# A mixture of experts whose tiles gather their rows: inverse slot map by one-hot products, W1 as the stationary operand, layer norms batch by batch

## The chip, the cores and the metric

The kernel runs on one core of a Trainium2 chip. The metric is the device time of one launch in microseconds (us). A core has five engines that run their own instruction streams in order and meet at semaphores: TensorE (PE), VectorE (DVE), ScalarE (ACT), GpSimd (POOL) and SyncE (SP), which here only issues DMAs. An engine that waits holds up all that stands behind the wait in its own stream.

## The reference

An audio tower of two layers over 8 sequences. The first stage keeps 16 of each 128 tokens, which leaves 8 x 512 = 4096 tokens of D = 128 numbers. Then (cut to what matters):

```python
h = h + L0_attn(layernorm(h), ...)          # gated retention
h = h + L0_ffn(layernorm(h), ...)           # experts, top 1
h = h + L1_attn(layernorm(h), video, ...)   # cross-attention
h = h + L1_ffn(layernorm(h), ...)           # experts, top 2

# L0_ffn: E = 8 experts, F = 512, one expert for each token, gate 1
logits = xf @ Wr + br;  idx = top_1(logits)
out[token] = relu(xf @ W1[idx] + b1[idx]) @ W2[idx] + b2[idx]

# L1_ffn: two experts for each token, gates = softmax of the two logits
h_e = relu(xf @ w1[e] + b1[e]) @ w2[e] + b2[e]
y_e = (xf + h_e - mean) * rsqrt(var + 1e-6) * gamma[e] + beta[e]
out[token] = gate_1 * y_e1 + gate_2 * y_e2
```

## The kernel before

The 4096 tokens lie in SBUF as G = 32 groups of 128 (`hidden`). The stages run one after the other with a barrier between them: the choice of tokens, `project` and the rest of the retention, the first mixture (moe1), the norm of the cross-attention (`crossnorm`) and the attention itself, the second mixture (moe2), and the end.

Both mixtures are one function, `route_and_mix`. Its first block, the **route**, takes the layer norm, the router's logits, the top 1 or 2, and the slot of each token: slots are grouped by expert and rounded up to tiles of 128, so that a tile has one expert. There are 40 tiles in moe1 and 72 in moe2. Then GpSimd scatters the 32 groups of normed rows (64 in moe2, once for each choice) to a DRAM table `routed`, in slot order, by indirect DMAs (L1064). Slots without a token need a row too, so `zero_dram` fills both tables with zeros earlier, during `project`. A row carries the slot of the output and the gate as two more columns.

`LayerNorm` works in phases: `statistics` of all 32 groups on VectorE (L201, L205), one power of 32 columns on GpSimd (L154), then `batch` for batch (L218). It is used by `project`, both routes and `crossnorm`.

The second block, the **mix**, runs the tiles. The ring holds RING = 8 tiles; SyncE loads pairs of tiles from `routed` (L1230), each pair as soon as the results that lay in its places are out, so up to eight tiles ahead. Every engine runs the tiles in an unrolled turn of 8, with the experts' numbers read into registers at a turn's start (`experts`). TensorE is in order. In its step t it transposes the rows of tile t+1 into `psX` (`turn_rows`, L1283), takes the first product of tile t into `psH` (L1278: the rows stationary, 512 columns of W1 moving), transposes the hidden numbers of tile t-1 into `psF` (L1288), and takes the second product of tile t-2 into `psY` (L1297). VectorE copies `psH` to `hid` (L1368), and in moe2 does `begin` of tile t-2 (L1382 to L1388: bias, residual, statistics) and `finish` of tile t-3 (L1395 to L1398), which sets `result_ready`. ScalarE copies the transposed rows (L1336) and does bias and relu (L1342). GpSimd takes the power of moe2's norm (L154) and scatters each result to DRAM (L1244).

The order on TensorE and on VectorE is what the steps of the prediction rest on:

```python
# TensorE, step t                    # VectorE, step t (moe2)
turn_rows(t + 1)                     # hidden_copy(t)
first_product(t)                     # begin(t - 2)   needs second_product(t - 2)
turn_hidden(t - 1)                   # finish(t - 3)  sets result_ready
second_product(t - 2)
```

## Time and profile before

| what | us |
|---|---|
| median of 2 runs (3289.16 and 3291.8) | 3290.48 |
| span of the profiled execution | 3251.5 |
| outside the span (the profiled execution's own time is taken as the median: 3290.48 - 3251.5) | 39.0 |
| PE busy | 2491.1 (77%) |
| DVE busy | 2290.4 (70%) |
| POOL busy | 1794.4 (55%) |
| ACT busy | 1729.9 (53%) |
| moe1: route with norm, scatter, mix | 53, 44, 140 |
| moe2: route with norm, scatter, mix | 55, 90, 336 |
| cross-attention after its norm | 1826 |

The span is the time from the first to the last instruction of one profiled execution. The shares are means over stages that stand apart by barriers, so the two mixtures have to be read by themselves: a window from a stage's start to its end gives the busy time of each engine there. PEclk is TensorE's granted clock as a share of its upper level: 0.50 is 1.2 GHz, 1.00 is 2.4 GHz. In a timeline, [x <-y] is the idle time of the engine before the row and what ended it; "issue" is a wait for nothing that the profile shows.

### The profile page before, as it was taken

The page shows a single profiled execution, that of the slowest core. Times are in us where ns is not written, and L with a number is a line of the kernel's source. Part 1 is how long each engine was busy: PE and PEld are TensorE (multiplying, and loading weights), DVE is VectorE, ACT ScalarE, POOL GpSimd, SP SyncE. Part 2 cuts the span into 40 slices and gives each one's busy share as a digit, 9 for nine tenths or more (in the row PEclk, how much of TensorE's full clock was granted, in tenths as well). Part 3 has the DMA queues.
Part 4 walks back from the last instruction along what each step waited for, and adds up shares of the span by engine and source line. Part 5 has one row for each costly group of instructions (what it writes and reads, how often), then busy time and mean ns, then how long its engine had stood idle before and what let it go on. Part 6 is the DMA issues. An engine that isn't in the chain of part 4 may idle for free. (4 is left out here: it accounts for less than half of the span.)

```text
span 3251.5 us, 57608 instructions
## 1 busy us (share of the span) xinstructions
PE 2491.1 (77%) x15032; PEld 2097.6 (65%) x15033; DVE 2290.4 (70%) x5410; ACT 1729.9 (53%) x3648; POOL 1794.4 (55%) x1986
## 2 busy tenths in 40 slices
PE   5441077528489999999999999999999997326663
PEld 3220055426368988898898889889888986214442
DVE  6624633413479999999999999999999997225664
ACT  2123122204257777777777777777777775113331
POOL 2325500133257777777777777777777775343332
PEclk8665555558789999999999999999999999568887
DMA  6260000211100000000000000000000001110103
GB/s 210 73 110 0 0 1 0 59 33 38 48 1 1 0 0 0 0 0 0 0 0 0 0 0 0 0 0 0 0 0 0 0 0 60 38 41 27 31 30 93
DMA packets 88587, 72.49 MB, mean 22 GB/s; under 512 B 21600, under 2 KB 75872, under 8 KB 88544
## 3 DMA queue, kind: packets, MB, share of 16 engines
q1 hardware_dynamic: 70480, 51.49, 6.3%
q0 software_dynamic: 7680, 15.84, 1.4%
q10 hardware_dynamic: 10384, 4.66, 0.5%
q8 instruction: 18, 0.29, 0.0%
q14 instruction: 25, 0.20, 0.0%
HBM read 48.66 MB, written 23.30 MB: 22 GB/s over the span
## 5 line engine op out<-in xcount | busy, mean ns | idle before, releaser
L1810 POOL TENSOR_TENSOR attend_weights<-attend_weights,attend_scales 128x512 f32<-128x512 f32 x1024 | 1068.9, 1044 | 499.5 <-DVE attend_scales L1721 471.9
L1713 DVE TENSOR_REDUCE attend_maxima<-attend_psL 128x8 fp32r<-128x512 f32 x1030 | 706.9, 686 | 146.0 <-PE attend_psL L1591 146.0
L1770 ACT ACTIVATE attend_highT<-attend_psT 128x512 fp32r<-128x512 f32 x1024 | 556.2, 595 | 261.9 <-PE attend_psT L1605 261.9
L1717 DVE TENSOR_REDUCE attend_sums<-attend_weights 128x8 f32<-128x512 f32 x1029 | 653.2, 635 | 3.2 <-ACT attend_weights L1766 3.2
L1766 ACT ACTIVATE attend_weights<-attend_psL 128x512 f32<-128x512 f32 x1029 | 615.9, 599 | 11.1 <-PE attend_psL L1595 11.1
L1605 PE MATMUL attend_psT<-consts,attend_weights 128*128 128x128 f32 x4096 | 530.4, 272 | 0.0
L1605 PEld LDWEIGHTS attend_psT<-consts,attend_weights 128*128 128x128 f32 x4096 | 479.1, 140 | 70.4 <-issue 0.2
L1615 PE MATMUL attend_psA<-attend_highT,attend_chunk_values 128*128 128x256 f32 x2048 | 515.6, 285 | 1.6
L1615 PE MATMUL attend_psA<-attend_lowT,attend_chunk_values 128*128 128x256 f32 x2048 | 513.6, 282 | 0.0
L1595 PE MATMUL attend_psL<-attend_maxima,neg_ident 128*128 128x512 f32 x1029 | 434.0, 422 | 3.9 <-DVE attend_maxima L1713 3.9
L1590 PE MATMUL attend_psL<-keys,attend_q_high 128*128 (+1 forms) x1030 | 411.1, 399 | 8.8 <-PE attend_psA L1615 7.2
L1591 PE MATMUL attend_psL<-keys,attend_q_low 128*128 (+1 forms) x1030 | 406.8, 395 | 0.0
L1615 PEld LDWEIGHTS attend_psA<-attend_lowT,attend_chunk_values 128*128 128x128 f32 x2048 | 389.4, 190 | 13.1
L1615 PEld LDWEIGHTS attend_psA<-attend_highT,attend_chunk_values 128*128 128x128 f32 x2048 | 389.9, 190 | 8.1 <-issue 8.1
L1774 ACT ACTIVATE attend_lowT<-attend_psT 128x512 fp32r<-128x512 f32 x512 | 306.4, 598 | 146.2 <-PE attend_psT L1641 146.2
L1725 DVE TENSOR_TENSOR attend_lowT<-attend_psT,attend_highT 128x512 fp32r<-128x512 f32 x512 | 348.7, 681 | 6.0 <-ACT attend_highT L1770 6.0
L1590 PEld LDWEIGHTS attend_psL<-keys,attend_q_high 128*128 128x128 f32 x1030 | 194.0, 188 | 58.7 <-issue 10.2
L1591 PEld LDWEIGHTS attend_psL<-keys,attend_q_low 128*128 128x128 f32 x1030 | 194.5, 189 | 37.1
L1641 PE MATMUL attend_psT<-attend_highT,neg_ident 128*128 128x512 f32 x512 | 202.6, 396 | 0.0
L1595 PEld LDWEIGHTS attend_psL<-attend_maxima,neg_ident 128*128 128x128 f32 x1029 | 195.2, 190 | 7.5 <-DVE attend_maxima L1713 7.5
L1721 DVE RECIPROCAL attend_scales<-attend_sums 128x8 f32<-128x8 f32 x1028 | 198.3, 193 | 0.0
L1824 POOL TENSOR_TENSOR attend_chunk_values<-values,attend_chunk_values 128x256 fp32r<-128x256 f32 x256 | 189.4, 740 | 0.0
(299 smaller groups left out, 3081.4 us busy)
## 6 DMA issues: line engine op xcount, KB each, us to landing
select_xbuf<-in_x_dram SPq DMA_DIRECT2D x16, 1024.0 KB, 5.4
routed<-project_zeros SPq DMA_DIRECT2D x14, 520.0 KB, 11.3
moe2mix_rows<-routed SPq DMA_DIRECT2D x36, 130.0 KB
select_emb<-L_attn_video_embeds_dram ACTq DMA_DIRECT2D x16, 256.0 KB, 2.9
moe2back_back<-result SPq DMA_DIRECT2D x8, 512.0 KB, 7.2
moe1mix_rows<-routed SPq DMA_DIRECT2D x20, 130.0 KB, 2.2
moe_w<-in_L_ffn_W_dram SPq DMA_DIRECT2D x1, 2048.0 KB, 10.8
moe1back_back<-result SPq DMA_DIRECT2D x4, 512.0 KB, 6.2
```

The costliest lines, as they stand in the source:

```text
L1590: pe.matmul(psL[:, s, :], q_high[h][:, tile], K.keys[:, ds(key, KC)], start=True, stop=False, skip_group_check=True)
L1591: pe.matmul(psL[:, s, :], q_low[h][:, tile], K.keys[:, ds(key, KC)], start=False, stop=False, skip_group_check=True).then_inc(logits_ready, 1)
L1595: pe.matmul(videos(psL[:, s, :]), K.neg_ident[:], maxima[:, s, :, None].to_broadcast([P, VC, FR]), start=False, stop=True, skip_group_chec ...
L1605: mm = pe.matmul(psT[:, side, at:at + P], weights[:, w + t, k * P:(k + 1) * P], ident, is_transpose=True, start=(at == 0), stop=False, ski ...
L1615: mm = pe.matmul(psA[:, j * 2 * P:(j + 1) * 2 * P], value, part[:, half, side, at], start=False, stop=(k == SUB - 1), skip_group_check=True)
L1713: dve.tensor_reduce(maxima[:, s, :], videos(psL[:, s, :]), X, ALU.max).then_inc(maxima_ready, 1)
L1717: dve.tensor_reduce(sums[:, w, :], videos(weights[:, w, :]), X, ALU.add).then_inc(summed, 1)
L1725: dve.tensor_tensor(lowT[:, half, LEFT, :], psT[:, LEFT, :], highT[:, half, LEFT, :].bitcast(F32), ALU.subtract).then_inc(left_lows, 1)
L1766: act.activation(weights[:, w, :], psL[:, w % TB, :], ACT.Exp, scale=float(DH1) ** -0.5).then_inc(exped, 1)
L1770: act.activation(highT[:, half, side, :], psT[:, side, :], ACT.Copy).then_inc(highs, 1)
L1774: act.activation(lowT[:, half, RIGHT, :], psT[:, RIGHT, :], ACT.Copy).then_inc(right_lows, 1)
L1810: pool.tensor_tensor(w, w, scales[:, s, :, None].to_broadcast([P, VC, FR]), ALU.mult).then_inc(normalised, 1)
```

## The change

It has three parts.

**Layer norms.** `statistics` and `batch` give way to `batches`: for each batch of four groups the statistics, the square, a power of four columns on GpSimd and the scaling, with the statistics of the next batch ahead of the scaling of this one. All four users take it. In `project` the wait for the weights now stands ahead of the norm.

**The route.** No row is scattered and nothing is filled with zeros. SyncE writes the normed table to DRAM in token order, by four plain DMAs (in moe2 behind the gates, which are its last two columns). Which token sits in which slot is found on the chip: for each four groups VectorE makes one-hots of the tile (`tile_token`, which carries the token's number) and of the lane (`lane_hot`), and TensorE multiplies them into `psI`, over 8 such parts in moe1 and 16 in moe2. Some operations on `psI` give `source` (the row to gather), `target` (the row of the result) and `second` (which of the two gates).

**The mix.** GpSimd gathers the rows of a tile from the table (L1225) and scatters the results (L1233). EARLY = 5 tiles are gathered first; the gather of tile t+5 stands behind the scatter of tile t, which waits for its result. SyncE loads nothing. ScalarE copies the tile's W1 (128x512) to `w1_tile`, TensorE takes the first product with W1 stationary in four matmuls, whose output is already transposed, so `psF`, `hid` and their copy are gone. In moe2 a fifth matmul of the second product adds the residual, the root is ScalarE's Sqrt with a reciprocal on VectorE, and the gate comes by one more small operation (L1374).

```diff
-        pool.wait_ge(self.square_ready, 1)
-        inverse_root(pool, K, self.root[:], self.square[:]).then_inc(self.root_ready, 1)
...
+        for b in range(B):
+            part = slice(b * TB, (b + 1) * TB)
+            pool.wait_ge(self.square_ready, b + 1)
+            inverse_root(pool, K, self.root[:, part], self.square[:, part]).then_inc(self.root_ready, 1)
+    def batches(self, dve, hidden, rows, ready, ring=B, used=None):
+        for b in range(B + 1):
+            if b < B:
+                for g in range(b * TB, (b + 1) * TB):
+                    dve.bn_stats(self.stats[:, g, :], hidden[:, g, :]).then_inc(self.steps, 1)
+            if b > 0:
+                dve.wait_ge(self.root_ready, b)
+                if used and b > ring:
+                    dve.wait_ge(used, b - ring + 2)
+                for g in range((b - 1) * TB, b * TB):
+                    ins = dve.tensor_scalar(rows[:, g % (ring * TB), 0:D], hidden[:, g, :], self.mv[:, g, 0:1], self.root[:, g:g + 1],
+                                            ALU.subtract, ALU.mult)
+                ins.then_inc(ready, 1)
+            if b < B:
+                dve.wait_ge(self.steps, b * 2 * TB + TB)
+                for g in range(b * TB, (b + 1) * TB):
+                    dve.bn_aggr(self.mv[:, g, :], self.stats[:, g, :]).then_inc(self.steps, 1)
+                dve.wait_ge(self.steps, (b + 1) * 2 * TB)
+                part = slice(b * TB, (b + 1) * TB)
+                dve.tensor_scalar(self.square[:, part], self.mv[:, part, 1], self.scale, self.eps, ALU.mult, ALU.add).then_inc(self.square_ready, 1)
...
+                    table = K.normed_dram[top].rearrange("(g p) d -> p g d", p=P)
+                    if last:
+                        sp.wait_ge(shares_kept, 2)
+                    for q in range(4):
+                        part = slice(q * (G // 4), (q + 1) * (G // 4))
+                        sp.wait_ge(norm_ready, 2 * (q + 1))
+                        sp.dma_start(table[:, part, :], normed[:, part, :]).then_inc(table_out, 16)
+                    sp.wait_ge(table_out, 64)
...
-                    pool.wait_ge(rows_kept, B + 2)
-                    for k in range(top):
-                        pool.wait_ge(slots_ready, k + 1)
-                        pool.wait_ge(tagged, 2 * (k + 1))
-                        for g in range(G):
-                            pool.indirect_dma_start(K.routed_dram[top], bass.IndirectOffsetOnAxis(ap=slots[:, k, g:g + 1], axis=0),
...
+                    for i in range(parts):
+                        k, n = i // (G // PART), i % (G // PART)
+                        pe.wait_ge(lanes_ready, i + 1)
+                        pe.wait_ge(tokens_ready, PART * (i + 1))
+                        for j in range(PART):
+                            mm = pe.matmul(psI[:, k, 0:tiles], lane_hot[:, i % HOTS, j, :], tile_token[:, i % HOTS, j, :],
+                                           start=(n == 0 and j == 0), stop=(n == G // PART - 1 and j == PART - 1))
+                        mm.then_inc(hots_used, 1)
...
+                    for i in range(parts):
+                        if i >= HOTS:
+                            dve.wait_ge(hots_used, i - HOTS + 1)
+                        for j in range(PART):
+                            c = i * PART + j
+                            dve.tensor_scalar(tile_token[:, i % HOTS, j, :], K.const("lane")[:, 0:tiles], tile_of[:, c:c + 1],
+                                              K.const("token1")[:, c % G:c % G + 1], ALU.is_equal, ALU.mult).then_inc(tokens_ready, 1)
+                        dve.tensor_tensor(lane_hot[:, i % HOTS], K.const("lane")[:, None, :].to_broadcast([P, PART, P]),
+                                          lane_of[:, i * PART:(i + 1) * PART, None].to_broadcast([P, PART, P]), ALU.is_equal).then_inc(lanes_ready, 1)
...
+                    spare = K.const("spare")[:, 0:tiles]
+                    dve.wait_ge(hots_used, parts)
+                    steps.then(dve.tensor_copy(token1[:], psI[:, 0, 0:tiles]))
+                    if last:
+                        steps.mark(dve.tensor_scalar(second[:], psI[:, 1, 0:tiles], 1.0, None, ALU.min))
+                        steps.then(dve.tensor_tensor(token1[:], psI[:, 1, 0:tiles], token1[:], ALU.add))
+                    steps.mark(dve.tensor_scalar(source[:], token1[:], -1.0, 0.0, ALU.add, ALU.max))
+                    steps.then(dve.tensor_scalar(filled[:], token1[:], 1.0, None, ALU.min))
+                    if last:
+                        steps.then(dve.scalar_tensor_tensor(token1[:], second[:], float(N), token1[:], ALU.mult, ALU.add))
+                    steps.then(dve.scalar_tensor_tensor(token1[:], token1[:], float(SPARE - 1), spare, ALU.add, ALU.subtract))
+                    steps.then(dve.tensor_tensor(token1[:], token1[:], filled[:], ALU.mult))
+                    steps.then(dve.tensor_tensor(target[:], token1[:], spare, ALU.add))
...
-            RING, PAIR = 8, 2
+            RING, EARLY = 8, 5
...
+                    def gather(t):
+                        pool.indirect_dma_start(rows[:, t % RING, :], None, K.normed_dram[top],
+                                                bass.IndirectOffsetOnAxis(ap=source[:, t:t + 1], axis=0)).then_inc(rows_in[t % RING], 16)
+                    for t in range(EARLY):
+                        gather(t)
+                    for t in range(tiles):
+                        pool.wait_ge(result_ready, t + 1)
+                        pool.indirect_dma_start(K.result_dram[top], bass.IndirectOffsetOnAxis(ap=target[:, t:t + 1], axis=0),
+                                                result[:, t % RING, :], None).then_inc(result_out[t % RING], 16)
+                        if t + EARLY < tiles:
+                            if t + EARLY >= RING:
+                                pool.wait_ge(result_out[(t + EARLY) % RING], 16 * ((t + EARLY) // RING))
+                            gather(t + EARLY)
...
-                    def first_product(t, s, e):
-                        pe.matmul(psH[:, s % 2, :], rowsT[:, s % 2, :], w1[:].rearrange("p e f -> p (e f)")[:, ds(e * F, F)],
-                                  start=True, stop=True).then_inc(hid_ready, 1)
...
+                    def first_product(t, s, bank_used):
+                        pe.wait_ge(w1_copied, t + 1)
+                        if bank_used:
+                            pe.wait_ge(hidT_done, t - 1)
                         for c in range(FC):
-                            mm = pe.transpose(psF[:, s % 2, c * P:(c + 1) * P], hid[:, s % 2, c * P:(c + 1) * P], ident)
-                        mm.then_inc(hidT_ready, 1)
+                            part = slice(c * P, (c + 1) * P)
+                            mm = pe.matmul(psH[:, s % 2, part], w1_tile[:, s % 2, part], rowsT[:, s % KEEP, :],
+                                           start=True, stop=True, skip_group_check=True)
+                        mm.then_inc(hid_ready, 1)
...
+                        if last:
+                            mm = pe.matmul(psY[:, s % 2, 0:D], rowsT[:, s % KEEP, :], ident, start=False, stop=True)
                         mm.then_inc(mixed_ready, 1)
...
+                        act.activation(rowsT[:, s % KEEP, :], psX[:, s % 2, 0:P], ACT.Copy).then_inc(rowsT_copied, 1)
+                        act.activation(w1_tile[:, s % 2, :], w1[:].rearrange("p e f -> p (e f)")[:, ds(e * F, F)], ACT.Copy).then_inc(w1_copied, 1)
+                    def activate(t, s, e, used):
+                        act.wait_ge(hid_ready, t + 1)
+                        if used:
+                            act.wait_ge(mixed_ready, t - 1)
...
+                            ins = act.activation(hidT[:, s % 2, c * P:(c + 1) * P], psH[:, s % 2, c * P:(c + 1) * P], ACT.Relu,
                                                  bias=flat[:, ds(e + c * E, 1)])
                         ins.then_inc(hidT_done, 1)
+                    def deviation(t, s):
+                        if last:
+                            act.wait_ge(square_ready, t + 1)
+                            act.activation(root[:, s % 2:s % 2 + 1], square[:, s % 2:s % 2 + 1], ACT.Sqrt).then_inc(root_ready, 1)
...
-                        dve.wait_ge(rows_in[s // PAIR], 16 * it + 16)
-                        steps.then(dve.tensor_tensor(res, rows[:, s, 0:D], of_expert(b2, e), ALU.add))
-                        dve.wait_ge(mixed_ready, t + 1)
-                        steps.then(dve.tensor_tensor(res, mixed, res, ALU.add))
+                        ins = dve.tensor_tensor(res, mixed, of_expert(b2, e), ALU.add)
+                        ins.then_inc(mixed_used, 1)
+                        dve.wait_ge(mixed_used, t + 1)
...
                         res = result[:, s, :]
+                        dve.wait_ge(root_ready, t + 1)
+                        steps.mark(dve.reciprocal(inverse[:], root[:, s % 2:s % 2 + 1]))
+                        steps.mark(dve.scalar_tensor_tensor(scale[:, s % 2:s % 2 + 1], second[:, ds(t, 1)], rows[:, s, D + 1:D + 2], rows[:, s, D:D + 1], ALU.mult, ALU.add))
                         steps.then(dve.scalar_tensor_tensor(res, res, mv[:, s % 2, 0:1], of_expert(gamma, e), ALU.subtract, ALU.mult))
-                        dve.wait_ge(root_ready, t + 1)
-                        steps.then(dve.scalar_tensor_tensor(res, res, root[:, s % 2:s % 2 + 1], of_expert(beta, e), ALU.mult, ALU.add))
-                        dve.tensor_scalar(res, res, rows[:, s, D + 1:D + 2], None, ALU.mult).then_inc(result_ready, 1)
+                        steps.then(dve.scalar_tensor_tensor(res, res, inverse[:], of_expert(beta, e), ALU.mult, ALU.add))
+                        dve.tensor_scalar(res, res, scale[:, s % 2:s % 2 + 1], None, ALU.mult).then_inc(result_ready, 1)
```

In the order of the built program one sees what stands in a row. The first place is GpSimd's stream in the mix of moe2, before (`result` at the left is the table of results in DRAM):

```order
L1244 DMA result<-moe2mix_result,moe2mix_rows 9216x128
L154 TENSOR_TENSOR moe2mix_root<-moe2mix_square,consts 128x1
L1244 DMA result<-moe2mix_result,moe2mix_rows 9216x128
L154 TENSOR_TENSOR moe2mix_root<-moe2mix_square,consts 128x1
L1244 DMA result<-moe2mix_result,moe2mix_rows 9216x128
L154 TENSOR_TENSOR moe2mix_root<-moe2mix_square,consts 128x1
```

and after, from the start of that block (`normed` is the table in DRAM, `moe2mix_rows` the ring of tiles):

```order
L1225 DMA moe2mix_rows<-normed,moe_source 128x130 x5
L1233 DMA result<-moe2mix_result,moe_target 9216x128
L1225 DMA moe2mix_rows<-normed,moe_source 128x130
L1233 DMA result<-moe2mix_result,moe_target 9216x128
L1225 DMA moe2mix_rows<-normed,moe_source 128x130
L1233 DMA result<-moe2mix_result,moe_target 9216x128
L1225 DMA moe2mix_rows<-normed,moe_source 128x130
```

The powers have left GpSimd; five gathers come first, and each later gather stands behind a scatter.

The second place is TensorE's step in the mix of moe2, before (an ISA row sets an address from a register):

```order
L1283 MATMUL moe2mix_psX<-consts,moe2mix_rows 128x128
L1278 ISA
L1278 MATMUL moe2mix_psH<-moe_w,moe2mix_rowsT 128x512
L1288 MATMUL moe2mix_psF<-consts,moe2mix_hid 128x128 x4
L1292 REGISTER_ALU
L1295 REGISTER_ALU
L1297 ISA
L1297 MATMUL moe2mix_psY<-moe_w,moe2mix_hidT 128x128
L1297 ISA
L1297 MATMUL moe2mix_psY<-moe_w,moe2mix_hidT 128x128
```

and after:

```order
L1247 MATMUL moe2mix_psX<-consts,moe2mix_rows 128x128
L1256 MATMUL moe2mix_psH<-moe2mix_rowsT,moe2mix_w_tile 128x128 x4
L1266 ISA
L1266 MATMUL moe2mix_psY<-moe_w,moe2mix_hidT 128x128
L1266 ISA
L1266 MATMUL moe2mix_psY<-moe_w,moe2mix_hidT 128x128
L1266 ISA
L1266 MATMUL moe2mix_psY<-moe_w,moe2mix_hidT 128x128
L1266 ISA
L1266 MATMUL moe2mix_psY<-moe_w,moe2mix_hidT 128x128
L1271 MATMUL moe2mix_psY<-consts,moe2mix_rowsT 128x128
```

The row of `psX` still stands ahead of everything else of its step; the four transposes are gone, the first product has four rows, and the second product ends with a fifth (L1271).

The third place is VectorE's step in the mix of moe2, before:

```order
L1368 COPY moe2mix_hid<-moe2mix_psH 128x512
L1382 ISA
L1382 TENSOR_TENSOR moe2mix_result<-moe2mix_rows,moe_b 128x128
L104 REGISTER_ALU
L1384 TENSOR_TENSOR moe2mix_result<-moe2mix_psY,moe2mix_result 128x128
L104 REGISTER_ALU
L1385 BN_STATS moe2mix_stats<-moe2mix_result 128x6
L104 REGISTER_ALU
L110 MEMSET moe2mix_pause 128x1
L1387 BN_AGGR moe2mix_mv<-moe2mix_stats 128x2
L104 REGISTER_ALU
L1388 TENSOR_SCALAR moe2mix_square<-moe2mix_mv 128x1
```

and after:

```order
L1359 TENSOR_TENSOR moe2mix_result<-moe2mix_psY,moe_b 128x128
L1362 BN_STATS moe2mix_stats<-moe2mix_result 128x6
L106 REGISTER_ALU
L112 MEMSET moe2mix_pause 128x1
L1364 BN_AGGR moe2mix_mv<-moe2mix_stats 128x2
L106 REGISTER_ALU
L1365 TENSOR_SCALAR moe2mix_square<-moe2mix_mv 128x1
L1373 RECIPROCAL moe2mix_inverse<-moe2mix_root 128x1
L1374 ISA
L1374 SCALAR_TENSOR_TENSOR moe2mix_scale<-moe_second,moe2mix_rows 128x1
L1375 REGISTER_ALU
L1375 SCALAR_TENSOR_TENSOR moe2mix_result<-moe2mix_result,moe2mix_mv,moe_gamma 128x128
```

The copy of the hidden numbers and the row of rows and bias (L1382) are gone; the reciprocal and the scale stand at the head of `finish`, which still comes behind the next tile's `begin`.

## Rows read from the trace of the kernel before

**Rows 1.** Busy time by stage; columns: us, PE, PEld, DVE, ACT, POOL, PEclk, DMA, GB/s

```profile
625.00:678.00 53.00, 24.56 (x160) 23.58 (x160) 27.01 (x121) 8.92 (x16) 5.73 (x2) 0.53 0.35 90
678.00:722.00 44.00, 0.00 (x0) 0.00 (x0) 0.20 (x2) 0.00 (x0) 30.46 (x32) 0.50 0.15 48
722.00:862.00 140.00, 105.42 (x600) 78.71 (x600) 39.35 (x80) 53.51 (x200) 46.68 (x80) 0.87 0.14 41
870.00:904.00 34.00, 8.92 (x32) 5.72 (x32) 19.95 (x98) 4.78 (x8) 5.46 (x1) 0.50 0.00 0
2747.00:2802.00 55.00, 24.89 (x160) 23.92 (x160) 29.53 (x130) 9.16 (x17) 5.42 (x1) 0.53 0.37 106
2802.00:2892.00 90.00, 0.00 (x0) 0.00 (x0) 3.02 (x9) 0.00 (x0) 61.38 (x64) 0.50 0.14 47
2892.00:3228.00 336.00, 213.92 (x1080) 148.60 (x1080) 192.83 (x720) 101.18 (x360) 115.17 (x144) 0.87 0.09 29
2998.80:3035.40 36.60, 25.11 (x121) 17.52 (x120) 21.47 (x80) 11.24 (x40) 12.80 (x16) 0.83 0.09 29
```

**Rows 2.** Timeline around the two scatters of rows; columns: start us, length us

```profile
677.69 1.07 POOL L1064 DMA_INDIRECT routed<-moe1route_normed,moe_slots  x1 [34.30 <-DVE moe_slots L1178]
...
716.95 0.96 POOL L1064 DMA_INDIRECT routed<-moe1route_normed,moe_slots  x1 [0.31 <-issue]
...
724.83 0.45 PE L1283 MATMUL moe1mix_psX<-consts,moe1mix_rows 128*128 128x128 f32 x1 [51.54 <-DMA moe1mix_rows<-routed]
...
2894.70 0.45 PE L1283 MATMUL moe2mix_psX<-consts,moe2mix_rows 128*128 128x128 f32 x1 [96.60 <-DMA moe2mix_rows<-routed]
```

**Rows 3.** Timeline of VectorE in moe1's layer norm and first routing step

```profile
625.93 1.01 DVE L201 BATCH_NORM_STATS2 moe1norm_stats<-hidden  x4 [1.18 <-PEq L176]
...
635.28 2.40 DVE L205 BATCH_NORM_AGGREGATE moe1norm_mv<-moe1norm_stats 128x2 f32<-128x6 f32 x32
...
643.88 2.30 DVE L218 TENSOR_SCALAR moe1norm_rows<-hidden,moe1norm_mv,moe1norm_root 128x128 f32 x8 [5.99 <-POOL moe1norm_root L154]
...
665.54 0.42 DVE L1121 TENSOR_TENSOR moe1route_logits<-moe1route_psR,moe1route_router_bias 128x256 f32<-128x256 f32 x1 [5.66 <-PE moe1route_psR L1085]
```

**Rows 4.** Timeline of TensorE in one turn of moe1's mix

```profile
751.71 0.47 PE L1283 MATMUL moe1mix_psX<-consts,moe1mix_rows 128*128 128x128 f32 x1 [4.54 <-issue]
...
753.71 1.06 PE L1288 MATMUL moe1mix_psF<-consts,moe1mix_hid 128*128 128x128 f32 x4
754.56 1.92 PE L1297 MATMUL moe1mix_psY<-moe_w,moe1mix_hidT 128*128 x8
...
759.07 0.27 PE L1283 MATMUL moe1mix_psX<-consts,moe1mix_rows 128*128 128x128 f32 x1
...
760.04 0.60 PE L1288 MATMUL moe1mix_psF<-consts,moe1mix_hid 128*128 128x128 f32 x4
760.48 1.06 PE L1297 MATMUL moe1mix_psY<-moe_w,moe1mix_hidT 128*128 x8
```

**Rows 5.** Timeline of one step of moe2's mix, all engines

```profile
2970.11 0.29 DVE L1384 TENSOR_TENSOR moe2mix_result<-moe2mix_psY,moe2mix_result 128x128 f32<-128x128 f32 x1 [0.71 <-PE moe2mix_psY L1297]
...
2971.95 0.29 DVE L1398 TENSOR_SCALAR moe2mix_result<-moe2mix_result,moe2mix_rows 128x128 f32<-128x128 f32 x1
...
2972.15 0.68 DVE L1368 COPY moe2mix_hid<-moe2mix_psH 128x512 f32<-128x512 f32 x1
2972.39 0.57 POOL L154 TENSOR_TENSOR moe2mix_root<-moe2mix_square,consts 128x1 f32<-128x1 f32 x1 [1.83 <-DVE moe2mix_result L1398]
...
2972.47 1.13 PE L1297 MATMUL moe2mix_psY<-moe_w,moe2mix_hidT 128*128 x8 [1.06 <-DVE moe2mix_result L1398]
...
2973.71 0.29 DVE L1384 TENSOR_TENSOR moe2mix_result<-moe2mix_psY,moe2mix_result 128x128 f32<-128x128 f32 x1 [0.68 <-PE moe2mix_psY L1297]
```

**Rows 6.** Waits in moe2's mix; columns: total us, times, longest

```profile
PE moe2mix_psY L1297 <- DVE moe2mix_result L1398: 46.5, 49, 3.0
```

**Rows 7.** Indirect DMA of moe2's mix, the view of the tile moe2mix_rows

```profile
DMA to landing us min/median/max: 2.2/2.3/3.5
```

313 lines of the change are left out of this document (110 added, 203 removed).

## Prediction

> **What bounds the kernel now.** I read the busy time by stage first [rows 1], because the whole-span shares (PE 77%) come mostly from the 1826 us of attention, which the change leaves alone. Four kinds of stage remain. In the routes (53 and 55 us) no engine is busy more than about half the time: a chain of small steps. In the two scatters (44 and 90 us) only GpSimd works, and everybody waits for it. In the mixes TensorE leads: 105.4 of 140 us in moe1; in moe2 213.9 of 336, with VectorE at 192.8. The timeline of a mix step [rows 5] shows why neither reaches its span in moe2: the second product waits for `result_ready` (the wait L1297 <- L1398 holds 46.5 us in 49 cases [rows 6]) and VectorE then waits for the product. The rows themselves are never late inside the mix, since SyncE loads them up to eight tiles ahead. This is the cover that I watch below.
>
> **Layer norms.** Before, in moe1's route: 32 statistics from 625.93, 32 aggregates in 2.40, a GpSimd power (5.99 idle), then scaling at 2.30 for 8, with waits, and the first logits step at 665.54: 39.6 us [rows 3]. After, VectorE needs for each batch 1.01 (statistics) + 0.30 (an eighth of 2.40) + about 0.2 (square) + 1.15 (half of 2.30) + about 0.45 for waits at semaphores = 3.1; the power of four columns lies beside the next batch's statistics. 8 x 3.1 = 24.8, and behind the last batch about 4 of the 5.66 us that VectorE waits there now: 28.8. That is -11, and the same in moe2. `crossnorm` and `project` have the same norm, but TensorE and ScalarE pace their batches and `project` now waits for its weights first: -7 each, an estimate, bounds 0 and -11. Sum -36. The zero fills lie beside `project` and cost or save nothing on the path.
>
> **Scatters become one-hots.** A scatter comes every (716.95 - 677.69) / 31 = 1.27 us, and the mix begins at 724.83, 47.1 after the first [rows 2]. Instead, each part costs VectorE one 128x512 operation (0.68, as L1368 [rows 5]) and four small ones on 128x40 or 128x72. Their price has no row; below it lies an aggregate's 0.075, above it 0.29 for 128x128 [rows 5]. I take 0.19 and 0.22, nearer the upper row: 1.44 and 1.55 a part, 11.5 us for 8 and 24.8 for 16 (bounds 7.8 to 14.7, and 15.7 to 29.4). The four matmuls of a part lie beside the next part; if each cost a quarter of the slow second product (1.92 / 4 = 0.48 [rows 4]) they would be the pace at 1.92, +4 and +6. Around them stand 0.8 for the digits, 1.3 for the owners, 1.6 (moe1) and 3.0 (moe2) for the tail, 1.2 for the block's change and 2.5 for the first gather. The slots are known 0.9 before moe1's first scatter (677.69 [rows 2]) and at about 2802.4 in moe2 [rows 1]. moe1's first `psX` comes at 676.8 - 0.5 + 0.8 + 11.5 + 1.3 + 1.6 + 1.2 + 2.5 = 695.2 against 724.83: -29.6. moe2's comes at 2802.4 + 0.9 + 24.8 + 1.3 + 3.0 + 1.2 + 2.5 = 2836.1 against 2894.70: -58.6. The table's write ends beside the one-hots. All savings: -124.
>
> **The mix of moe2, where the gathers now stand.** Loads left SyncE, which had nothing else to do, and stand in GpSimd's stream, one gather behind one scatter. Follow a tile. The gather of tile r+5 is issued after the scatter of tile r, and that waits for result r. Result r is `finish` in VectorE's step r+3, behind `begin` of tile r+1 in the same step. `begin` needs the second product of tile r+1, which TensorE does in its step r+3, behind `turn_rows` of tile r+4. So the rows of r+5 are not even requested until the rows of r+4 have arrived and gone through three engines. Five early tiles are exactly as many as one result needs; none is left to run ahead. TensorE's wait for rows holds its first and second products; VectorE, ScalarE and GpSimd wait behind those. One tile costs one whole round:
>
> - result to scatter 0.15 (the next GpSimd step starts at 2972.39, L1398 ends at 2972.24 [rows 5]); scatter to gather 1.27 [rows 2];
> - gather to landing 2.5: an indirect DMA here has 2.2 / 2.3 / 3.5 [rows 7], and a gather reads before it writes, so I go a little above the median; bounds 2.2 and 3.5;
> - TensorE's step, with a hand-over of 0.1 before and after. At the clock's upper level a step lasts from 759.07 to 761.54, 2.47 us, less 0.44 for `psF` (760.04 to 760.48) = 2.03, and the fifth matmul adds 0.27: 2.3. At the lower level it lasts from 751.71 to 756.48, 4.77, less 0.85 for `psF` (753.71 to 754.56) = 3.92, plus 0.43: 4.35 [rows 4];
> - VectorE from L1384 at 2970.11 to the end of L1398 at 2972.24: 2.13 [rows 5], plus 0.25 for reciprocal and scale: 2.4.
>
> The round is 0.15 + 1.27 + 2.5 + 0.1 + 4.35 + 0.1 + 2.4 = 10.9 us at the lower level and 8.8 at the upper. The registers' loads at a turn's start (4.54 idle in [rows 4]) now lie inside the wait, as does all of ScalarE's added work: the copy of W1 lies beside the wait for rows, and uncovered it would cost about 0.6 a tile, 43 us in all. Which level? The clock was granted at 0.53 and 0.50 in the stages where TensorE works less than half the time (24.6 of 53, 8.9 of 34) and at 0.83 in a mix turn with 25.1 of 36.6 [rows 1]; the new step keeps it busy 4.35 of 10.9 or 2.3 of 8.8. The step after a wait of 4.54 us ran at the lower level [rows 4], and each new step follows a wait of 6.5. I take the lower.
>
> The Trainium skill, page "TensorE: Matmul & The Clock Gate", section "HAM oscillation — how this bites in real kernels", says that where the matmuls of each tile are shorter than the wait for its data, the clock drops in every wait and each tile starts cold. The step after the idle 4.54 us agrees [rows 4]. By that rule moe2's mix would go at 10.9 a tile; without it at 8.8.
>
> Before: 9 turns x 36.6 = 329 [rows 1]. After: 67 rounds x 10.9 = 730, some 15 until the first result and 12 for the last four tiles = 757. So +428 (at the upper level 67 x 8.8 + 24 = 614, +285).
>
> **The mix of moe1.** The result is set in `begin` of step r+2, so it needs the rows of r+3 and not of r+4: two tiles share a round. At the lower level 3.92 + 0.1 + 0.29 + 0.2 + 1.27 + 2.5 + 0.1 = 8.4 for two, at the upper 6.5. 17.5 rounds = 147, ends 12, uncovered turn loads 4: 163, against 140 - 12 = 128 [rows 1]. +35 (upper level about +5).
>
> One table load for Sqrt on ScalarE is under 2 us. **Sum**, from the profiled 3251.5 + 39.0 = 3290.5, which is the median: -124 + 35 + 428 = 3630.
>
> **Rivals.**
> - *A, the forecast: lockstep, lower clock*, 3630. For it: the order of the three streams, and the clock rows.
> - *B: lockstep, but the clock stays at its upper level*: -124 + 5 + 285 = 3457 to 3470. For it: mix stages had 0.87 as a mean. Against: that was with TensorE busy two thirds of the time.
> - *C, the other side: no lockstep*. If five tiles in flight cover the round trip, each tile takes what the busiest engine needs: GpSimd two DMAs, 2.54, VectorE 2.4, TensorE 2.3. Then moe2 goes at moe1's old pace, 9 x 26.2 + 12 = 248 (-77; 26.2 is moe1's turn of 8, (140 - 9) / 5 [rows 1]), moe1 -9, and the kernel takes 3080. The place is the gather's start: it needs gather r+5 to be issued while tile r+4 is still under way. The point from which it decides: the change is slower once moe2 pays over (124 + 329) / 72 = 6.3 us a tile, and DMAs, TensorE and VectorE in series are above that even with every lower bound (0.15 + 1.27 + 2.2 + 2.3 + 2.1 = 8.0). Against it: in-order streams leave no way past the wait.
> - *D: the table does not do what it says*, with gathers at the slow end, 3.5 a landing: +67, 3700.
>
> **Chances.** A 0.62, B 0.20, C 0.07, D 0.04; the rest (a clock between the levels, a partly broken chain) 0.07, mostly slower. The range takes in A, B's upper part and the gather's bounds: 3455 to 3700. Faster by over 2% (about what a measurement can tell from no change) 0.07, within 2% 0.02, slower 0.91.
>
> **What would show it.** In moe2's mix L1247 starts about 10.9 apart, each behind a wait for the DMA of `moe2mix_rows` of 6 us or so; L1233 waits for VectorE's L1377; PEclk is near 0.5; the first `psX` of moe2's mix comes some 58 us sooner after the route's start plus 11. In moe1's mix the rows arrive in pairs. The forecast is wrong if TensorE's waits for those DMAs are short, or if PEclk in the mix is near 1.

## The result and the profile after

The changed kernel took 3602.13 us (median of 3577.7 and 3626.56) against 3290.48: a ratio of 1.099, 95% interval 1.074 to 1.125. The profiled execution took 3577.7 us with a span of 3575.8. Executions of one kernel fall into two groups some 40 us apart (before: 3246 to 3261 or 3279 to 3296), by TensorE's clock in the `project` stage, which the last section shows; both profiled executions, before and after, had the higher clock there, so their spans, 3251.5 and 3575.8, are compared below: +324.3.

The windows of the stages after the change answer to [rows 1] (same columns: us, busy of PE, PEld, DVE, ACT and POOL, PEclk, DMA share, GB/s). They are moe1's norm, its route behind the norm, its mix; the norm of the cross-attention; the same three of moe2; and eight tiles in the middle of moe2's mix:

```profile
612.40:640.00 27.60, 21.18 (x96) 20.12 (x96) 19.17 (x107) 4.78 (x8) 8.07 (x8) 0.50 0.87 232
640.00:669.40 29.40, 12.65 (x96) 11.32 (x96) 20.36 (x71) 0.00 (x0) 2.00 (x2) 0.56 0.06 18
669.40:833.80 164.40, 99.48 (x680) 93.79 (x680) 11.66 (x40) 75.35 (x240) 76.23 (x78) 0.88 0.12 32
853.50:879.00 25.50, 8.92 (x32) 5.72 (x32) 19.28 (x105) 4.78 (x8) 8.09 (x8) 0.50 0.00 0
2722.00:2749.70 27.70, 21.17 (x96) 20.11 (x96) 19.27 (x108) 4.78 (x8) 8.08 (x8) 0.55 0.75 210
2749.70:2797.50 47.80, 21.55 (x128) 18.89 (x128) 39.19 (x129) 0.23 (x1) 2.07 (x3) 0.54 0.24 46
2797.50:3547.50 750.00, 282.47 (x1368) 267.72 (x1368) 144.87 (x720) 148.57 (x505) 138.82 (x142) 0.63 0.05 13
3100.00:3184.00 84.00, 31.96 (x152) 30.29 (x152) 14.90 (x73) 15.14 (x51) 15.65 (x16) 0.62 0.05 13
```

The scatter stages are gone (29.5 and 47.9 us lie between the logits and the first rows in place of 59.3 and 107.6), and moe2's mix has grown to 750 us, in which no engine is busy even 40% of the time. TensorE's clock there is 0.63, where it was 0.87 [rows 1]. The timeline shows one tile of moe2's mix:

```profile
3101.24 0.99 POOL L1233 DMA_INDIRECT result<-moe2mix_result,moe_target  x1 [8.62 <-DVE moe2mix_result L1377]
3102.53 0.97 POOL L1225 DMA_INDIRECT moe2mix_rows<-normed,moe_source  x1 [0.30 <-issue]
...
3105.06 0.48 PE L1247 MATMUL moe2mix_psX<-consts,moe2mix_rows 128*128 128x128 f32 x1 [6.52 <-DMA moe2mix_rows<-normed,moe_source]
...
3105.33 1.92 PE L1256 MATMUL moe2mix_psH<-moe2mix_rowsT,moe2mix_w_tile 128*128 128x128 f32 x8
...
3107.03 1.91 PE L1266 MATMUL moe2mix_psY<-moe_w,moe2mix_hidT 128*128 x8
...
3108.74 0.64 PE L1271 MATMUL moe2mix_psY<-consts,moe2mix_rowsT 128*128 128x128 f32 x2
...
3109.52 0.29 DVE L1359 TENSOR_TENSOR moe2mix_result<-moe2mix_psY,moe_b 128x128 f32<-128x128 f32 x1 [8.56 <-PE moe2mix_psY L1271]
...
3111.51 0.29 DVE L1377 TENSOR_SCALAR moe2mix_result<-moe2mix_result,moe2mix_scale 128x128 f32<-128x128 f32 x1
3112.07 0.99 POOL L1233 DMA_INDIRECT result<-moe2mix_result,moe_target  x1 [8.57 <-DVE moe2mix_result L1377]
```

From one scatter to the next are 10.83 us. They go: scatter and gather issued 1.29 apart, rows used at 3105.06 (2.53 after the gather), TensorE until 3109.38, VectorE until 3111.80, and 0.27 to the next scatter. No two of these overlap. Before, a step took 3.60 (L1384 to L1384 [rows 5]). The view of waits in the same stage (engine and instruction, what it waited for, total us, times, longest) shows all engines in it:

```profile
DVE moe2mix_result L1359 <- PE moe2mix_psY L1271: 586.6, 69, 14.6
POOL result L1233 <- DVE moe2mix_result L1377: 579.8, 71, 12.0
PE moe2mix_psX L1247 <- DMA moe2mix_rows<-normed,moe_source: 462.7, 68, 8.0
```

The gathers themselves are nearly as fast as the scatters (the view of `moe2mix_rows`, where [rows 7] had 2.2, 2.3 and 3.5 for the scatters):

```profile
DMA to landing us min/median/max: 2.4/2.5/3.6
```

In moe1 the scatters come in pairs, two tiles to a round (GpSimd's timeline; the gathers between them are left out). The first round shown, from 688.13 to 694.86, lasts 6.73; the next, which holds the register loads at a turn's start, 10.54:

```profile
688.13 0.99 POOL L1233 DMA_INDIRECT result<-moe1mix_result,moe_target  x1 [3.50 <-DVE moe1mix_result L1356]
...
690.70 0.99 POOL L1233 DMA_INDIRECT result<-moe1mix_result,moe_target  x1 [0.30 <-issue]
...
694.86 0.99 POOL L1233 DMA_INDIRECT result<-moe1mix_result,moe_target  x1 [1.89 <-DVE moe1mix_result L1356]
...
697.48 0.98 POOL L1233 DMA_INDIRECT result<-moe1mix_result,moe_target  x1 [0.36 <-issue]
...
705.40 0.99 POOL L1233 DMA_INDIRECT result<-moe1mix_result,moe_target  x1 [5.66 <-DVE moe1mix_result L1356]
```

Stage by stage, from the first to the last instruction named:

| stretch | before | after | difference | forecast |
|---|---|---|---|---|
| start to moe1's norm | 625.9 | 612.7 | -13.2 | -7 |
| moe1's norm to its logits | 39.6 | 27.3 | -12.3 | -11 |
| moe1's logits to the first `psX` | 59.3 | 29.5 | -29.8 | -29.6 |
| moe1's mix, first `psX` to last scatter | 128.1 | 163.3 | +35.2 | +35 |
| to the norm of the cross-attention | 18.0 | 21.2 | +3.2 | 0 |
| that norm to the attention's first product | 33.7 | 25.6 | -8.1 | -7 |
| attention, to moe2's norm | 1842.9 | 1842.8 | -0.1 | 0 |
| moe2's norm to its logits | 39.6 | 27.3 | -12.3 | -11 |
| moe2's logits to the first `psX` | 107.6 | 47.9 | -59.7 | -58.6 |
| moe2's mix | 325.2 | 748.8 | +423.6 | +428 |
| the end | 31.6 | 29.4 | -2.2 | 0 |

### The profile page after: what moved, and what is told of

Its sections match the earlier page's. It is cut to its first block and busy times, and to the rows that moved or that the text cites. A ratio compares the mean times of both kernels' runs of the same rounds, so it can differ in the third digit from the quotient of the medians.

```text
span 3575.8 us, 57595 instructions
## 1 busy us (share of the span) xinstructions
PE 2567.8 (72%) x15496; PEld 2243.6 (63%) x15497; DVE 2255.1 (63%) x5536; ACT 1791.8 (50%) x3817; POOL 1770.4 (50%) x1917
## 5 line engine op out<-in xcount | busy, mean ns | idle before, releaser
L1359 DVE TENSOR_TENSOR moe2mix_result<-moe2mix_psY,moe_b 128x128 f32<-128x128 f32 x72 | 21.0, 291 | 588.3 <-PE moe2mix_psY L1271 586.6
L1247 PE MATMUL moe2mix_psX<-consts,moe2mix_rows 128*128 128x128 f32 x72 | 32.4, 450 | 465.3 <-DMA moe2mix_rows<-normed,moe_source 462.7
L1233 POOL DMA_INDIRECT result<-moe2mix_result,moe_target x72 | 71.1, 987 | 590.0 <-DVE moe2mix_result L1377 579.8
L1247 PEld LDWEIGHTS moe2mix_psX<-consts,moe2mix_rows 128*128 128x128 f32 x72 | 13.2, 183 | 479.5 <-issue 382.1
L1305 ACT ACTIVATE moe2mix_rowsT<-moe2mix_psX 128x128 f32<-128x128 f32 x72 | 20.0, 278 | 435.5 <-PE moe2mix_psX L1247 433.2
L1560 PEld LDWEIGHTS attend_psL<-keys,attend_q_high 128*128 128x128 f32 x1030 | 194.0, 188 | 58.9 <-issue 10.3
## 6 DMA issues: line engine op xcount, KB each, us to landing
moe_w<-in_L_ffn_W_dram SPq DMA_DIRECT2D x1, 2048.0 KB, 10.8
moe_w<-in_L_ffn_w_dram SPq DMA_DIRECT2D x1, 2048.0 KB, 10.8
```

The costliest lines, as they stand in the source:

```text
L1560: pe.matmul(psL[:, s, :], q_high[h][:, tile], K.keys[:, ds(key, KC)], start=True, stop=False, skip_group_check=True)
```

## The experiments

All start from the changed kernel unless said otherwise, and compute the same result. "Mix" is the time from the first `psX` of the mixture to its last scatter, from the profiled execution, so it is free of the 40 us of `project`; kernels with one execution are to be compared by their mixes and not by the last column.

| kernel | moe1 mix | moe2 mix | time (ratio to before, 95% interval) |
|---|---|---|---|
| before | 128.1 | 325.2 | 3290.5 |
| changed | 163.3 | 748.8 | 3602.1 (1.099, 1.074 to 1.125) |
| e1: EARLY 4 and 6 | 329.0 | 380.7 | 3376.5, one execution |
| e2: EARLY 7 | 138.0 | 303.9 | 3150.0 (0.957, 0.944 to 0.970) |
| e3: finish first | 168.2 | 436.4 | 3311.8, one |
| e5: rows last | 155.0 | 465.7 | 3330.6, one |
| e4, e6, e10: fill of 20, 40, 56 | 163.0, 162.1, 163.2 | 729.7, 722.7, 708.1 | 3598.5, 3600.2, 3576.9, one each |
| e8: before with the new products | 117.9 | 289.2 | 3210.3, one |
| e7: EARLY 7 and finish first | 116.8 | 247.1 | 3030.4, one |
| e9: ring of 12 (10) | 135.1 | 283.2 | 3128.1 (0.952, 0.942 to 0.961) |
| e11: ring of 12 and finish first | 110.8 | 238.7 | 3060.0 (0.933, 0.922 to 0.943) |
| e12: e9 once more | 110.9 | 218.8 | 3039.6 (0.925, 0.914 to 0.936) |

**How many tiles ahead (e1, e2).** The theory is a count: a result of moe2 needs the rows of four tiles later and one of moe1 of three, so EARLY - 4 tiles share a round in moe2 and EARLY - 3 in moe1 (one and two in the changed kernel). The rival is that the new mix is slow by what it does.

```diff
-            RING, EARLY = 8, 5
+            RING, EARLY = 8, (6 if last else 4)
```

> The changed kernel with EARLY = 4 in moe1 and 6 in moe2 instead of 5 in both; nothing else differs. Theory (the gather of tile t+EARLY stands behind result t, and result t needs the rows of t+3 in moe1 and of t+4 in moe2): moe1 now pays a whole round for each tile, 40 x 8.2 = about 320 us from its first psX to its last scatter instead of 163.3; moe2 now has two tiles in a round, 34 rounds x 10.9 plus some 25 at the ends and up to 20 of uncovered register loads = 350 to 420 us instead of 748.8. Rival 1 (the new mix is slow by what it does: two indirect DMAs, the copy of W1, Sqrt, whatever the order): EARLY changes nothing, 163 and 749. Rival 2 (a gather is slow because several DMAs are under way at once): moe2 gets no better with more tiles in flight, and moe1 gets better with fewer.

Measured: 329.0 and 380.7. One kernel moved both mixes by the count, in opposite directions; the work of each tile was unchanged. The landings stayed at a median of 2.5 in moe2, so rival 2 falls too.

```diff
-            RING, EARLY = 8, 5
+            RING, EARLY = 8, 7
```

> The changed kernel with EARLY = 7 in both mixtures. Theory: three tiles of moe2 share a round of about 10.9, so the pace comes near to that of the busiest engine: 255 to 300 us for the mix of moe2 (748.8 with EARLY = 5, 325.2 before), and 110 to 130 us for moe1 (163.3 with 5, 128.0 before). The whole kernel at about 3576 - 470 - 45 = 3060 us, faster than before by some 6%. Rival 1 (the work itself is slow): 749 and 163, 3576 in all. Rival 2 (more DMAs under way make each slower): moe2 above 400 with landings well over 2.5 us.

Measured: 138.0 and 303.9, each a little above its range, and 3150.0 in all where 3060 was expected; the kernel is 4.3% faster than before. GpSimd's timeline has the three tiles of a round (scatters only):

```profile
2922.01 0.99 POOL L1233 DMA_INDIRECT result<-moe2mix_result,moe_target  x1 [4.08 <-DVE moe2mix_result L1377]
...
2924.57 0.99 POOL L1233 DMA_INDIRECT result<-moe2mix_result,moe_target  x1 [0.30 <-issue]
...
2927.15 0.99 POOL L1233 DMA_INDIRECT result<-moe2mix_result,moe_target  x1 [0.32 <-issue]
...
2933.48 0.99 POOL L1233 DMA_INDIRECT result<-moe2mix_result,moe_target  x1 [4.06 <-DVE moe2mix_result L1377]
```

Three scatters 2.57 apart, as fast as GpSimd issues two DMAs each, then a pause; from 2922.01 to 2933.48 is one round, 11.5. The trace has two kinds of further waits, whose shares I did not price: the loads of the registers, which now lie open (one wait of TensorE at a turn's start is 5.87), and waits that the program by itself does not explain (39 us, summed over ScalarE and VectorE in both mixes; see e12).

**Which instructions tie the result to the rows (e3, e5).** If the chain is the one of the prediction, cutting it at either of two places must free one tile, with EARLY left at 5.

```diff
-                            begin(t - 2, (s - 2) % RING, e[s + 1])
                             finish(t - 3, (s - 3) % RING, e[s])
+                            begin(t - 2, (s - 2) % RING, e[s + 1])
```

> The changed kernel, EARLY = 5, but on VectorE finish of tile t-3 stands ahead of begin of tile t-2. Theory: result t then needs the rows of t+3 only, so moe2 has two tiles in a round. The round gets a little longer (the root of the tile comes after ScalarE's relu: 0.28 + 1.27 + 2.5 + 0.1 + 4.35 + 0.1 + 3.1 = 11.7), so 36 x 11.7 plus some 20 = about 440 us for the mix of moe2, or 350 if TensorE's clock comes up; moe1 stays at 163. Rival (the order on VectorE does not matter, the gathers do): 749, or more, since each step then waits for the root.

Measured: 436.4, with 440 forecast. moe1, which has no `finish` and the same instructions as in the changed kernel, took 168.2 (163.3 there), which shows how far one mix can differ between two executions.

```diff
-                            if s < RING - 1:
-                                turn_rows(s + 1, it)
-                            elif not closing:
-                                turn_rows(0, it + 1)
                             first_product(t, s, s >= 2 or not opening)
                             if s >= 2 or not opening:
                                 second_product(t - 2, ...)
+                            if s < RING - 1:
+                                turn_rows(s + 1, it)
+                            elif not closing:
+                                turn_rows(0, it + 1)
```

> The changed kernel, EARLY = 5, but in TensorE's step the rows of tile t+1 are transposed last, behind both products. Theory: result t then needs the rows of t+3 only, so two tiles of moe2 share a round; the round is longer, since ScalarE's copies of the rows and of W1 now lie on it (0.28 + 1.27 + 2.5 + 0.1 + 0.5 + 1.1 + 4.1 + 0.1 + 2.4 = 12.3): about 36 x 12.3 plus 20 = 460 us for the mix of moe2, or 370 with a higher clock. In moe1 result t then needs the rows of t+2: three tiles a round, but a longer step; 135 to 165. Rival (the place of the transpose does not matter): 749.

Measured: 465.7 and 155.0, as expected. Both links of the chain, `begin` ahead of `finish` and `turn_rows` ahead of the products, hold; either edit alone takes over 280 us off the mix.

**The clock's share (e4, e6, e10).** Forecast and rival B differ only in the level at which TensorE's step runs, and the rounds of the changed kernel last 10.2 to 12.4, never 8.8. The three kernels fill the wait for rows with transposes of the identity into a bank of PSUM that nobody reads.

```diff
+                            if last:
+                                for z in range(FILL):      # 20, 40, 56
+                                    pe.transpose(psZ[:, 0:P], ident, ident)
                             if s < RING - 1:
                                 turn_rows(s + 1, it)
```

> The changed kernel, EARLY = 5, with 20 transposes of the identity into a spare PSUM bank ahead of turn_rows in each step of moe2's mix; they compute nothing that is used, and lie inside the 6.5 us in which TensorE waits for rows. Theory A (the round has TensorE's step at the lower clock, 4.5 us, because it comes after the wait): the clock comes up, the step falls to 2.3 to 2.5 and the round from 10.85 to about 8.8: some 610 us for the mix of moe2 instead of 748.8. If the clock of the steps is not set by how long TensorE is idle ahead of them, the mix stays at 749. If the fill is longer than the wait, the mix gets longer.

Measured: 729.7. The expectation of 610 fell: the 20 ran at the upper clock behind the products, 2.35 us, and left 4.4 idle.

> As e4_fill, with 40 transposes of the identity instead of 20. There the 20 took only 2.35 us, because they ran behind the products when the clock had come up, and 4.4 us of idle time were left ahead of the next rows; the step began at the lower clock again (mix 729.7 instead of 748.8). If the idle time is what takes the clock down, 40 of them leave some 2 us idle and the round falls to about 8.8: 600 to 640 us. If the step's own work decides whatever comes ahead of it: 720 to 750.

Measured: 722.7, so the expected 600 to 640 fell. TensorE is now busy 77% of the mix. The step behind a wait of about 2 us came out either way. Of the 54 steps behind a wait of 1.8 us or more, 20 ran wholly at the upper level, 22 slowed down on the way, and 12 had their whole first product at the lower. Here is one that slowed down and one, three rounds later, that did not (TensorE's timeline):

```profile
3104.31 4.68 PE L1286 MATMUL moe2mix_psZ<-consts 128*128 128x128 f32 x40
3110.97 0.33 PE L1248 MATMUL moe2mix_psX<-consts,moe2mix_rows 128*128 128x128 f32 x1 [1.98 <-DMA moe2mix_rows<-normed,moe_source]
3111.14 1.67 PE L1257 MATMUL moe2mix_psH<-moe2mix_rowsT,moe2mix_w_tile 128*128 128x128 f32 x8
3112.60 1.92 PE L1267 MATMUL moe2mix_psY<-moe_w,moe2mix_hidT 128*128 x8
...
3114.73 4.59 PE L1286 MATMUL moe2mix_psZ<-consts 128*128 128x128 f32 x40
...
3142.55 0.33 PE L1248 MATMUL moe2mix_psX<-consts,moe2mix_rows 128*128 128x128 f32 x1 [2.27 <-DMA moe2mix_rows<-normed,moe_source]
3142.71 1.06 PE L1257 MATMUL moe2mix_psH<-moe2mix_rowsT,moe2mix_w_tile 128*128 128x128 f32 x8
```

> As e6_fill40, with 56 transposes of the identity, which at the 0.117 us that one took there last 6.6 us and cover the whole wait for rows. With 40 the idle time before the rows was 2.0 us and the step behind it still ran mostly at the lower clock (722.7 for the mix). If any idle time of 2 us is what takes the clock down, none is left now, the step runs at the upper clock and lasts 2.4 instead of 4.5, and a round takes about 9.0: some 630 us for the mix of moe2. If something in the step itself keeps the clock down, or if the fill runs at the lower clock and becomes longer than the wait: 720 or more.

Measured: 708.1 in all, but the rounds themselves became what was expected:

```profile
3105.34 6.28 PE L1286 MATMUL moe2mix_psZ<-consts 128*128 128x128 f32 x56
3112.02 0.33 PE L1248 MATMUL moe2mix_psX<-consts,moe2mix_rows 128*128 128x128 f32 x1 [0.40 <-DMA moe2mix_rows<-normed,moe_source]
3112.18 1.06 PE L1257 MATMUL moe2mix_psH<-moe2mix_rowsT,moe2mix_w_tile 128*128 128x128 f32 x8
3113.08 1.06 PE L1267 MATMUL moe2mix_psY<-moe_w,moe2mix_hidT 128*128 x8
3113.98 0.39 PE L1272 MATMUL moe2mix_psY<-consts,moe2mix_rowsT 128*128 128x128 f32 x2
3114.20 6.28 PE L1286 MATMUL moe2mix_psZ<-consts 128*128 128x128 f32 x56
3120.85 0.33 PE L1248 MATMUL moe2mix_psX<-consts,moe2mix_rows 128*128 128x128 f32 x1 [0.37 <-DMA moe2mix_rows<-normed,moe_source]
```

With 0.4 us idle the four matmul groups run at the upper clock: 3112.02 to 3120.85 is 8.83, where the prediction's rival B had 8.8. Seven rounds of a turn are mostly 8.8 to 9.0. The eighth is 14.3 to 15.9: the loads of the registers (mostly 4.3) are no longer covered when the fill stands behind them, and behind that idle time the fill itself runs at the lower level for a good part, up to 9.2 us for the 56 in place of 6.28. 7 x 8.9 + 15.3 = 77.6 a turn, nine turns, 698, against 708.1 measured. So a mix's total is no measure of the clock here, since the fill brings a cost of its own; the rounds are.

The rounds of the changed kernel last 10.8 on average and those of e10 8.9, so the lower clock cost about 1.9 us a round, some 130 us in all (an estimate, 67 x 1.9), and the lockstep the rest of the loss. All 67 steps behind a wait in the changed kernel (6.5 us or more each) have their first product at the lower level, 1.91 to 2.04 where the upper has 1.06; in 35 of them the clock came up within the second product. In such a round it falls again only within the wait: the round at 3148.58 has 0.50 until 3150.8, 1.00 from 3152.3 to 3154, and 0.50 again from 3156. That is why PEclk is 0.63 over the stage and not 0.5. In e10 no step behind a wait (0.35 to 1.8 us) ran at the lower level. So the lower level comes with the idle time ahead of a step, but its length alone does not decide: behind about 2 us both outcomes stand side by side (e6), and in moe1's mix of the changed kernel, where TensorE is busy about 60% of the time, 8 of the 11 steps behind a wait for rows of 2.0 to 2.9 us ran wholly at the upper level. What decides between them is open. The Trainium skill, page "TensorE: Matmul & The Clock Gate", section "HAM oscillation — how this bites in real kernels", has the same pattern from waits for data, and the trace agrees with it in every round of moe2's mix in the changed kernel.

**The rearranged products by themselves (e8).** The kernel before with the new TensorE, ScalarE and VectorE work in its mix; norms, scatters, and SyncE's loads of pairs stay. In short:

```diff
-                        pe.matmul(psH[:, s % 2, :], rowsT[:, s % 2, :], w1[...][:, ds(e * F, F)], ...)
+                            mm = pe.matmul(psH[:, s % 2, part], w1_tile[:, s % 2, part], rowsT[:, s % KEEP, :], ...)
...
-                    with pool.Fori(1, turns) as it:
-                        for s in range(RING):
-                            step(it * RING + s, s)
+                    for t in range(tiles):
+                        pool.wait_ge(result_ready, t + 1)
+                        pool.indirect_dma_start(K.result_dram[top], ..., result[:, t % RING, :], None)
```

> The kernel before with the changed mix (W1 stationary, its copy on ScalarE, the residual on TensorE, Sqrt and reciprocal), but its rows still scattered to slot order and loaded by SyncE; layer norms and route as before. It tells what the rearranged products are worth when rows are never late. Theory: they are no loss. TensorE's step in moe2 is 2.45 at the upper clock and its register loads 5.4 a turn, so a turn of 8 takes 26 to 29 us instead of 36.6: 240 to 275 us for the mix of moe2 (325.2 before); moe1 at 110 to 128 (128.0 before). Rival (the rearrangement is part of the loss): moe2 above 340.

Measured: 289.2 and 117.9, so a gain of 36.0 and 10.2; moe2's mix was above the range of 240 to 275. TensorE waits longer for rows than before. The second row is that of the kernel before:

```profile
PE moe2mix_psX L1253 <- DMA moe2mix_rows<-routed: 142.4, 17, 97.0
PE moe2mix_psX L1283 <- DMA moe2mix_rows<-routed: 110.9, 22, 96.6
```

97.0 of the 142.4 is the scatter stage, as 96.6 of the 110.9 was before, so inside the mix TensorE waits 45.4 us in place of 14.3. That the tiles now pass faster than a pair comes back would explain it, but no run tests it. The products are no part of the loss.

**Both edits, and a longer ring (e7, e9, e11, e12).** e7 joins the edits of e2 and e3.

> EARLY = 7 and finish ahead of begin together, ring of 8. Theory: four tiles of moe2 share a round (result t needs the rows of t+3, and the gather of t+7 stands behind it), so the waits for rows mostly go and the loads of the registers at a turn's start remain: 275 to 300 us for the mix of moe2 (303.9 with EARLY = 7 alone, 436.4 with finish first alone); moe1 as in e2_early7, 138. Rival: the two edits act on the same wait and do not add, 304 or more, since each step waits longer for the root.

Measured: 247.1 and 116.8, better than expected in both; 3030.4 us for the one execution. moe1 has the same instructions as in e2 and took 21 us less, a difference that e12 takes up.

```diff
-            RING, EARLY = 8, 5
-            assert RING <= E
+            RING = 12 if last else 10
+            EARLY = RING - 1
```

> The changed kernel with a ring of 12 tiles in moe2 and 10 in moe1 (turns of the same length) and EARLY = ring - 1. Theory: a gather now stands behind the result of 11 (9) tiles earlier, 7 (6) more than a result needs, so the round trip is hidden and the busiest engine with the loads of the registers sets the pace (TensorE 12 x 2.45 + 6.5 for a turn of 12, GpSimd 2.56 a tile): 225 to 260 us for the mix of moe2, 105 to 125 for moe1. The whole at 3000 to 3040, against 3144 with EARLY = 7.

Measured: 283.2, 135.1 and 3128.1 in all, each above its range. The edit also makes a turn longer, so that the registers are loaded six times in moe2 and four in moe1 in place of nine and five; no run parts this from the longer lead of the gathers. The view of waits has a releaser here that the other kernels but e2 lack, e.g. in moe2:

```profile
ACT moe2mix_hidT L1315 <- remote: 50.1, 19, 5.0
DVE moe2mix_result L1359 <- remote: 40.0, 11, 17.1
```

> The ring of 12 (10 in moe1) with EARLY = ring - 1, and finish ahead of begin. Theory: in e9_ring12 the rows are never late any more, so how many tiles a result needs makes no difference now: 280 to 290 us for the mix of moe2 as there (283.2), and the whole kernel within 0.5% of e9_ring12. Rival: the order on VectorE matters by itself, through the root that is needed sooner: slower by 10 us or more.

Measured: 238.7 and 110.8. "Within 0.5% of e9" fell, by 68 us, but 24 of them lie in moe1, whose instruction streams are the same in e9 and e11. So the comparison of the two says nothing certain of the order on VectorE, and the last run repeated e9:

> The kernel of e9_ring12 once more, unchanged. There and in e2_early7 ScalarE and VectorE sometimes waited some 3 us for a matmul that the trace shows as ended (released by 'remote' in the view of waits: 124 us in e9_ring12, 39 in e2_early7, none in the other runs), in moe1 too, whose instructions are the same in e11_ring12_finish, where moe1 took 110.8 instead of 135.1. Theory 1 (the stalls belong to the execution or the chip, not to the order on VectorE): they are absent this time in at least some of the executions, moe1's mix takes 110 to 117 and moe2's about 240 to 250, the whole 3060 to 3080. Theory 2 (they belong to this program): 135 and 283 again, about 3128.

Measured: 218.8 and 110.9, 3039.6 us: the same kernel, 88 us faster on another chip, without a single wait of that kind, as theory 1 has it; moe2's mix came out below the 240 to 250 that it gave. With a ring of 12 the original order on VectorE is at least no worse than finish first (218.8 and 238.7, on two chips, so the 20 us are not settled). The longer ring with the changed kernel's own order is 4.8% faster than the kernel before in e9 and 7.5% in e12.

## Why the prediction was right

The forecast was 3630, the median is 3602.13, inside the range of 3455 to 3700 and near the likeliest case. The mechanism was the one described; two of its terms, moe1's mix and the one-hots, came out right because errors cancelled.

- *Layer norms, -36.* Measured -12.3, -12.3, -8.1 and -13.2: -45.9. The batch costs 2.73 (from one L212 to the next), not 3.1, as VectorE's timeline in moe1's route shows, 0.35 of it the wait for the power, which I had taken as hidden, and the other waits smaller than estimated:

```profile
616.79 0.87 DVE L205 BATCH_NORM_STATS2 moe1norm_stats<-hidden 128x6 f32<-128x128 f32 x4
618.02 1.11 DVE L212 TENSOR_SCALAR moe1route_normed<-hidden,moe1norm_mv,moe1norm_root 128x128 f32<-128x128 f32 x4 [0.35 <-POOL moe1norm_root L156]
...
620.74 1.11 DVE L212 TENSOR_SCALAR moe1route_normed<-hidden,moe1norm_mv,moe1norm_root 128x128 f32<-128x128 f32 x4 [0.35 <-POOL moe1norm_root L156]
...
651.45 0.94 DVE L1165 TENSOR_SCALAR moe1route_tile_token<-consts,moe1route_tile_of 128x40 fp32r<-128x40 f32 x4
652.30 0.68 DVE L1167 TENSOR_TENSOR moe1route_lane_hot<-consts,moe1route_lane_of 128x512 fp32r<-128x512 f32 x1
652.90 0.93 DVE L1165 TENSOR_SCALAR moe1route_tile_token<-consts,moe1route_tile_of 128x40 fp32r<-128x40 f32 x4
```

The same view has the one-hots: 0.94 for four and 0.68 for the wide one, and the next part 1.45 after the last. In `project` the gain was about twice the estimate of 7; I took its batches to be paced by others, and the start of the stage mattered more: ScalarE's first copy of normed rows there starts at 201.70 in place of 210.39, 8.7 of the 13.2. The zero fills, which I put at nothing, left the same stage (DMA share from 188 to 267 us 0.58 before, 0.02 after), and no run prices them by themselves.
- *Scatters, -88.2.* Measured -89.5. The unrowed price of a 128x40 operation, taken as 0.19 between bounds of 0.075 and 0.29, is about 0.235 for each of four (0.94). The rows of one part overlap by some 0.17, which I had not taken off, and the two errors cancel: 1.44 was forecast for a part and 1.45 measured, in moe2 1.55 and 1.52. TensorE's products were never the pace.
- *The lockstep.* Shown by e1, e2, e3 and e5: the count of tiles in a round follows EARLY and each of the two orders. The round of 10.9 was 10.83 in the tile shown and 10.2 to 12.4 over all; its terms were 0.15 (0.27), 1.27 (1.29), 2.5 (2.53 to the first matmul, so 2.5 + 0.1 was 0.07 too much), 4.35 (4.32) and 2.4 + 0.1 for its hand-over (2.42). The bounds of the landing were not needed.
- *The clock.* I gave two reasons for the lower level. That each step follows a wait [rows 4] was the right one in kind: e10 takes the wait away, and the level goes with it, 2.0 in the round shown and 1.9 on average, where the prediction had 2.1. That TensorE is busy less than half the time [rows 1] was a weak one: in e6 TensorE was busy 77% of the mix, and 34 of 54 steps behind a wait still ran at the lower level in whole or in part. The sign "PEclk near 0.5" was missed, 0.63, since the clock came up within about half of the steps.
- *moe1, +35.* Measured +35.2, two tiles a round, but the terms were wrong and cancelled, so the number was luck. I took the lower level throughout, 8.4 for each round, and 4 us for all turn loads. PEclk was 0.88. The 14 rounds without a turn load took 6.7 to 9.4 from scatter to scatter, 7.6 on average, and the four with one 10.3 to 10.9, so the loads cost about 3 each, 12 in all. The clock of moe2's mix could not be carried over to moe1's.
- *What was wrong:* the 39.0 us "outside the span" of the kernel before. There are none: after the change 1.9 us lie outside it. The profiled execution of before had the higher clock in `project` (0.78), and the two timed ones, 38 to 40 us longer, by their time the lower. With like against like the change costs 324 us (the profiled executions) or 336 (3626.56 - 3290.48), against 312 by the medians. The forecast of the change, +339.5, stands on the stage times and is not touched. That rows were never late inside the mix of before was not so either: outside the scatter stage TensorE waited 14.3 us for them (110.9 - 96.6, shown at e8). And rival C's -77 for moe2 should have been -81, from 329 to 248.
- *Rival C* needed the gathers to run free. The longer ring gives that: moe2's mix at 218.8 to 283.2 (C had 248), moe1's at 110.8 to 135.1 (C had 119), and the whole at 3039.6, where C had 3080.
